# Scores of a batch's sixteen heads: fp32 matmuls of 64 rows, two heads side by side, in place of high and low parts

## The chip, the cores and the metric

The kernel runs on one core of one Trainium2 chip. The time is the device time of one execution in microseconds (us). Engines: PE (TensorE), DVE (VectorE), ACT (ScalarE), POOL (GpSimd) and SP (SyncE, which here only issues DMAs). PSUM is used as eight banks of 128 partitions x 512 fp32 numbers, named F0 to F3, S0, S1, TB and OB.

## The reference

Eight batches of 512 tokens x 128 channels go through two layers. The change touches only the last part, `_L1_ffn_ref`, an attention with 16 heads of 64 channels. Cut to what matters:

```python
q = jnp.einsum('btc,hdc->bhtd', x, Wq)
k = jnp.einsum('btc,hdc->bhtd', x, Wk)
...
v = jnp.einsum('bthe,bted->bhtd', mix_v, proj_v)
scores = jnp.einsum('bhid,bhjd->bhij', q * scale, k)
probs = jax.nn.softmax(scores, axis=-1)
attn = jnp.einsum('bhij,bhjd->bihd', probs, v)
...
res = jnp.einsum('bthe,bthd,efd->bthf', mask_o, attn, Wo)
return res.sum(axis=2)
```

Before it come, per batch, a linear attention with an MLP (`attn0`), eight dense experts (`moe_in`, `experts`), a causal attention with 8 heads (`attn1`) and the gates of this last part (`gates`).

## The kernel before, in words

Each engine runs its own program, and semaphores tie them. A program is a list of stages, each cut into marks; `schedule` walks a main stage's marks and puts marks of other stages beside them, in proportion. In the loop over batches two such walks follow each other. In the first, the **heads stage**, the 64 head steps of one batch (`heads`: 4 blocks of 128 query tokens x 16 heads) run beside `attn1` and `gates` of the next batch and `load`, `attn0` and `moe_in` of the one after. In the second, the **values stage**, `experts` runs beside the end of the heads (`finish`, `close`), the values and keys (`values`) and the first query steps (`begin`). The last batch has its values, and then its heads, with nothing beside them.

`head_steps` (line 63) writes the order of the steps: a *head* step per head and block, and other turns between them at places set by `QUERIES_AT`, `BACK_AT`, `MIXED_AT` and `RESULT_AT`:
- *queries* computes 128 tokens' queries of 8 heads into a bank (L971);
- *back* transposes 8 heads' results back (L984), DVE divides them (L1544), and after each second one SP sends them to DRAM (`out_rows`) and back in another layout (`onR`);
- two *mixed* turns (L991) add up the heads by their masks into `ymT` (L1209), and *result* (L997) multiplies by the output weights.

Every step but a rest takes the next of the two score banks S0 and S1 in turn (`TURN`). In `steps`, PE does at step k, in this order: the work of step k; for the head m of step k-2 the four transpositions of its exponentials `pr` into TB, called **T(m)** below (L719); and, if the head of step k-3 is odd, **AV** for that pair of heads (L1016), eight matmuls that alternate between the two column halves of OB, so that each head writes 64 partitions. ACT at step k first copies the transposed exponentials of step k-2 to `prT` (L1180), then computes the exponentials of head m, exp(m) (L1202). DVE gives it the negated maximum of the scores (L1529). Before PE fills a bank, it waits until what is in it has been read: for a head's scores, the exponential of the head two turns earlier.

A head's channels are 64 rows, but its score matmuls use all 128. Keys and queries are each split into a high part, rounded to fp32r, and a low part, the rest. One row half of `keys[:, h]` holds the high part and the other the low part of the same head. `q_high` holds the high part of the queries in both halves, `q_low` their low part in both, so two fp32r matmuls (L979 and L980) add up all four products:

```python
pe.matmul(bank_k[:, :], q_high[:, j % 3, h2, :], keys[:, h, :], start=True, stop=False)
pe.matmul(bank_k[:, :], q_low[:, j % 3, h2, :], keys[:, h, :], start=False, stop=True).then_inc(s_ps[0], 1)
```

For that, ACT copies the high part of the queries out of the bank (L1193, two copies of 64 rows), DVE subtracts it to give the low part (L1535, two), and two steps later ACT copies both parts to the other row half (L1186, four). For the keys, ACT copies the high part of two heads (L1147) and DVE subtracts into the other half (L1501), in each fourth mark of `values`, where DVE also multiplies (L1487) and adds up (L1495) the values. The experts' own DVE step is L1389, their matmuls L831, L834 and L839.

## Time and profile before

| what | value |
|---|---|
| median of 3 runs | 3120.25 us (3118.91 to 3121.88) |
| the profiled execution's own time | 3122.04 us |
| its span, first to last instruction | 3120.1 us |
| PE matmul busy | 2548.0 us, 82% |
| DVE, ACT, POOL busy | 1751.7, 1613.9, 788.4 us |
| mean granted clock of TensorE | 0.911 of 2.4 GHz |

The median is 1.8 us under the profiled execution, whose rows are used below. Busy time is the union of an engine's records; the ends of matmuls are modelled, so a busy PE need not be at its peak, and the distance between two starts says more than a duration. An fp32 matmul shows as two records, an fp32r matmul or an fp32 transposition as one.

### The profile page before, as it was taken

How to read it: one execution, taken by the hardware profiler on the slowest of the kernel's cores; microseconds unless marked ns; L12 is line 12 of the kernel's file. 1: busy time of each engine (PE TensorE's matmuls, PEld its weight loads, DVE VectorE, ACT ScalarE, POOL GpSimd, SP SyncE). 2: the span in 40 equal slices, each digit the busy share in tenths (PEclk: the TensorE clock that was granted, in tenths of full speed). 3: DMA queues.
4: the chain of work that ended last, by engine and by line, in shares of the span. 5: the costliest groups of instructions: out<-in, count | busy, mean ns of one | idle time of the engine just before them, and what ended most of it. 6: DMA issues, size and time to landing. Idle time of an engine off the chain costs nothing.

```text
span 3120.1 us, 44672 instructions
## 1 busy us (share of the span) xinstructions
PE 2548.0 (82%) x14892; PEld 1689.8 (54%) x14892; DVE 1751.7 (56%) x2906; ACT 1613.9 (52%) x3329; POOL 788.4 (25%) x370
## 2 busy tenths in 40 slices
PE   3984698789797997889787897979979797996487
PEld 2453347664476545765376644765457553774265
DVE  4235763547645494465935567364854649447732
ACT  0241246663566636664366635666366643774474
POOL 1003520106401181013601055011810127004500
PEclk7996799999898998999999998999989999998698
DMA  2110010102001120012101020011200121001001
GB/s 73 47 41 8 10 51 1 55 14 76 12 15 41 41 59 2 15 55 55 32 1 47 22 65 22 9 48 41 59 2 15 48 55 38 15 15 39 0 28 31
DMA packets 210739, 101.63 MB, mean 33 GB/s; under 512 B 137367, under 2 KB 189620, under 8 KB 210492
## 3 DMA queue, kind: packets, MB, share of 16 engines
q1 hardware_dynamic: 205052, 95.74, 11.1%
q10 hardware_dynamic: 5440, 2.75, 0.3%
q8 instruction: 136, 2.23, 0.3%
q14 instruction: 111, 0.91, 0.1%
HBM read 77.48 MB, written 20.99 MB: 32 GB/s over the span
## 4 chain that ended last, share of the span: by engine, by line
PE 61%; DVE 14%; issue 14%; ACT 8%; POOL 2%; DMA 1%; DVEq 0%; ACTq 0%; POOLq 0%; SPq 0%
PE bank L719 9%; PE bank L834 6%; PE bank L1016 6%; PE bank L831 6%; PE bank L839 6%; PE bank L871 5%; PE bank L979 4%; PE bank L887 4%; PE bank L980 3%; DVE vals L1495 2%; PE bank L997 2%; ACT pr L1202 2%; DVE prod L1487 2%; DVE nrm_o L1304 2%; DVE nmax L1529 1%
## 5 line engine op out<-in xcount | busy, mean ns | idle before, releaser
L704 POOL TENSOR_TENSOR prod<-pv,mixv 128x1024 f32<-128x1024 f32 x184 | 589.8, 3234 | 305.4 <-ACT pv L1141 157.1
L1529 DVE TENSOR_REDUCE nmax<-bank 128x1 f32<-128x512 f32 x512 | 351.0, 690 | 539.9 <-PE bank L980 519.3
L1202 ACT ACTIVATE pr<-bank,nmax 128x512 f32<-128x512 f32 x512 | 350.7, 685 | 189.3 <-DVE nmax L1529 187.6
L1180 ACT ACTIVATE prT<-bank 128x512 f32<-128x512 f32 x512 | 305.0, 596 | 258.0 <-PE bank L719 251.8
L643 POOL TENSOR_TENSOR rstd<-vareps,minus_half 128x4 f32<-128x4 f32 x48 | 50.0, 1043 | 1495.5 <-DVE vareps L1299 1495.4
L1083 ACT ACTIVATE arena<-bank 128x512 f32<-128x512 f32 x256 | 152.8, 597 | 444.3 <-PE bank L831 397.3
L979 PE MATMUL bank<-keys,q_high 128*128 128x512 f32 x512 | 267.6, 523 | 113.3 <-DVE on L1544 30.9
L719 PE MATMUL bank<-ident,pr 128*128 128x128 f32 x2048 | 327.1, 284 | 29.0 <-ACT prT L1180 28.6
L719 PEld LDWEIGHTS bank<-ident,pr 128*128 128x128 f32 x2048 | 256.9, 146 | 118.8 <-ACT prT L1180 41.9
L1495 DVE TENSOR_REDUCE vals<-prod 128x128 f32<-128x1024 f32 x256 | 306.9, 1209 | 11.7 <-POOL prod L704 10.8
L834 PE MATMUL bank<-h1T,Wu 128*128 128x512 f32 x512 | 272.1, 614 | 40.0 <-DVE arena L1389 39.9
L1016 PE MATMUL bank<-prT,vals 128*64 128x128 f32 x4096 | 299.2, 290 | 5.6 <-ACT prT L1180 5.6
L1389 DVE TENSOR_TENSOR arena<-bank,arena 128x512 f32<-128x512 f32 x256 | 175.0, 688 | 218.7 <-PE bank L834 192.8
L839 PE MATMUL bank<-arena,Wd 128*128 128x512 f32 x512 | 273.4, 620 | 27.0 <-DVE arena L1389 27.0
L831 PE MATMUL bank<-h1T,Wg 128*128 128x512 f32 x512 | 269.0, 607 | 3.9 <-ACT h1T L1048 3.9
L1417 DVE TENSOR_REDUCE nmax<-bank 128x1 f32<-128x128 f32 (+3 forms) x256 | 125.1, 491 | 251.1 <-PE bank L872 250.5
L1016 PEld LDWEIGHTS bank<-prT,vals 128*64 128x64 f32 x4096 | 234.4, 143 | 55.3 <-issue 40.7
L871 PE MATMUL bank<-arena,attT 128*128 128x512 f32 (+3 forms) x512 | 203.7, 482 | 14.3 <-ACT arena L1111 12.9
L980 PE MATMUL bank<-keys,q_low 128*128 128x512 f32 x512 | 214.3, 419 | 0.0
L979 PEld LDWEIGHTS bank<-keys,q_high 128*128 128x128 f32 x512 | 102.4, 200 | 189.3 <-ACT pr L1202 61.0
L834 PEld LDWEIGHTS bank<-h1T,Wu 128*128 128x128 f32 x512 | 97.3, 195 | 173.2 <-issue 105.9
L1487 DVE TENSOR_TENSOR prod<-pv,mixv 128x1024 f32<-128x1024 f32 x72 | 187.4, 2603 | 0.0
(226 smaller groups left out, 3878.0 us busy)
## 6 DMA issues: line engine op xcount, KB each, us to landing
Wg<-in_L_ffn_Wg SPq DMA_DIRECT2D x64, 256.0 KB, 2.9
Wu<-in_L_ffn_Wu SPq DMA_DIRECT2D x64, 256.0 KB, 3.5
Wd<-in_L_ffn_Wd SPq DMA_DIRECT2D x64, 256.0 KB, 3.9
out_rows<-on SPq DMA_DIRECT2D x32, 512.0 KB, 2.6
onR<-out_rows SPq DMA_DIRECT2D x32, 512.0 KB, 3.9
xin<-in_L_attn_x SPq DMA_DIRECT2D x8, 256.0 KB, 4.3
mask_rows<-masko SPq DMA_DIRECT2D x8, 256.0 KB, 4.6
maskR<-mask_rows SPq DMA_DIRECT2D x8, 256.0 KB, 6.6
```

Source lines behind the costliest of these rows:

```text
L704: g.tensor_tensor(*value_piece(n), ALU.mult).then_inc(vprod_r[0], 1)
L719: last = pe.transpose(dst[:, i * P:(i + 1) * P], src(i), ident[:, :])
L831: pe.matmul(F0[:, :], Wg[:, e % 2, j * P:(j + 1) * P], hbT[:, :], start=True, stop=True).then_inc(gu_g[0], 1)
L834: pe.matmul((F2, F3)[n % 2][:, :], Wu[:, e % 2, j * P:(j + 1) * P], hbT[:, :], start=True, stop=True).then_inc(gu_u[0], 1)
L839: pe.matmul(F1[:, :], Wd[:, e % 2, j, :], act[:, m % 3, :], start=(m == 0), stop=(m == n_all - 1)).then_inc(down_ps[0], 1)
L871: pe.matmul(f[:, 0:w], q1T[:, i * P:(i + 1) * P], k1z[:, h, 0:w], start=True, stop=False, skip_group_check=True)
L979: pe.matmul(bank_k[:, :], q_high[:, j % 3, h2, :], keys[:, h, :], start=True, stop=False)
L980: pe.matmul(bank_k[:, :], q_low[:, j % 3, h2, :], keys[:, h, :], start=False, stop=True).then_inc(s_ps[0], 1)
L1016: last = pe.matmul(OB[DS * odd:DS * odd + DS, at:at + P], vals[:, j, h - 1 + odd, :], prT[:, (m - 1 + odd) % 3, j * P:(j + 1) * P], start= ...
L1202: s.activation(pr[:, x % 2, :], bank_k[:, :], ACT.Exp, bias=nmax[:, x % 2:x % 2 + 1], accum_out=den[:, i % 2, h:h + 1]).then_inc(s_out[0], 1)
L1495: v.tensor_reduce(vals[:, i, HQ * q:HQ * q + HQ, :], prod[:, m % NPROD, :].rearrange("p (h d e) -> p h d e", h=HQ, e=NE), X_AXIS, ALU.add) ...
L1529: v.tensor_reduce(nmax[:, m % 2:m % 2 + 1], (S0, S1)[turn % 2][:, :], X_AXIS, ALU.max, negate=True).then_inc(nmax_r[0], 1)
```

## The change

It drops the high and low parts. `keys` now has one row half per head (fp32, 8 pairs of heads), `qs` likewise, so that both are plain copies of a bank of 128 rows. The scores of heads 2p and 2p+1 are one fp32 matmul each of 64 contraction rows, on the upper and the lower row half, the first into one score bank and the second into the other. PE issues both at the step of the even head, after it has waited for both banks; the step of the odd head issues no scores. The constants of the order change too.

```diff
-QUERIES_AT = (8, 11)
-BACK_AT = (13, 5)
-MIXED_AT = (9, 10)
+QUERIES_AT = (4, 8)
+BACK_AT = (14, 6)
+MIXED_AT = 10
...
-        keys = sb("keys", [P, HS, T], F32R)
-        q_high = sb("q_high", [P, 3, HS // 2, P], F32R)
-        q_low = sb("q_low", [P, 3, HS // 2, P], F32R)
+        keys = sb("keys", [P, NP, T])
+        qs = sb("qs", [P, 3, NP // 2, P])
...
+                    if kind == "head":
+                        for odd in range(0 if x % 2 else 2):
+                            free(b, turn + odd)
+                    elif kind != "rest":
+                        free(b, turn)
...
-                        pe.matmul(bank_k[:, :], q_high[:, j % 3, h2, :], keys[:, h, :], start=True, stop=False)
-                        pe.matmul(bank_k[:, :], q_low[:, j % 3, h2, :], keys[:, h, :], start=False, stop=True).then_inc(s_ps[0], 1)
+                    if kind == "head" and x % 2 == 0:
+                        i, p = x // HS, x % HS // 2
+                        j, r = 2 * i + p // (NP // 2), p % (NP // 2)
+                        if r == 0:
+                            wait(pe, s_out, b, COPIED[STEP_AT["queries", j]])
+                        for odd in range(2):
+                            half = slice(DS * odd, DS * odd + DS)
+                            pe.matmul((S0, S1)[(turn + odd) % 2][:, :], qs[half, j % 3, r, :], keys[half, p, :], start=True, stop=True).then_inc(s_ps[0], 1)
...
-                        for odd in range(2):
-                            r = DS * odd
-                            s.activation(keys[r:r + DS, 2 * p + odd, :], (TB, OB)[p % 2][r:r + DS, :], ACT.Copy).then_inc(kh_r[0], 1)
+                        s.activation(keys[:, p, :], (TB, OB)[p % 2][:, :], ACT.Copy).then_inc(keys_r[0], 1)
...
-                        for part in (q_high, q_low):
-                            for odd in range(2):
-                                last = s.activation(other_half(part, x, odd), own_half(part, x, odd), ACT.Copy)
-                        last.then_inc(q_both[0], 1)
...
-                        for odd in range(2):
-                            last = s.activation(own_half(q_high, x, odd), queries_of(bank_k, odd), ACT.Copy)
-                        last.then_inc(s_out[0], 1)
+                        s.activation(qs[:, x % 3, :, :].rearrange("p a t -> p (a t)"), bank_k[:, :], ACT.Copy).then_inc(s_out[0], 1)
...
-                            last = v.tensor_tensor(keys[DS - r:2 * DS - r, 2 * p + odd, :], (TB, OB)[p % 2][r:r + DS, :], keys[r:r + DS, 2 * p + odd, :], ALU.subtract)
...
-                            last = v.tensor_tensor(own_half(q_low, m, odd), queries_of((S0, S1)[turn % 2], odd), own_half(q_high, m, odd), ALU.subtract)
```

`free(b, turn)` is the wait for the bank's earlier contents, as before but without the low part. DVE now handles a *back* turn ahead of the maximum of the same step, not behind it. Lines of the changed kernel have other numbers.

PE, heads stage of the last batch, two heads in a row before the change (L719 is T, L1016 is AV):

```order
L979 MATMUL bank<-keys,q_high 128x512
L980 MATMUL bank<-keys,q_low 128x512
L719 MATMUL bank<-ident,pr 128x128 x4
L979 MATMUL bank<-keys,q_high 128x512
L980 MATMUL bank<-keys,q_low 128x512
L719 MATMUL bank<-ident,pr 128x128 x4
L1016 MATMUL bank<-prT,vals 64x128 x8
```

The same place after it (L972 scores, L705 T, L1008 AV, L976 a turn back):

```order
L972 MATMUL bank<-keys,qs 128x512 x2
L705 MATMUL bank<-ident,pr 128x128 x4
L1008 MATMUL bank<-prT,vals 64x128 x8
L705 MATMUL bank<-ident,pr 128x128 x4
L972 MATMUL bank<-keys,qs 128x512 x2
L705 MATMUL bank<-ident,pr 128x128 x4
L1008 MATMUL bank<-prT,vals 64x128 x8
L705 MATMUL bank<-ident,pr 128x128 x4
L976 MATMUL bank<-ident,oaT 128x128 x4
```

Scores stood between the two transpositions; now only AV does, and both heads' scores stand together.

SP, first DMAs of the heads stage inside the loop, before (`out_rows` and `onR` are the head rows of blocks 0 and 1, `xin` and `rows` belong to the load of a later batch):

```order
L578 DMA out_rows<-on 128x1024
L281 ISA
L580 DMA onR<-out_rows 128x16x64
L281 REGISTER_ALU
L578 DMA out_rows<-on 128x1024
L281 REGISTER_ALU
L580 DMA onR<-out_rows 128x16x64
L281 REGISTER_ALU
L554 ISA
L554 DMA xin<-in_L_attn_x 128x4x128
L557 ISA
L557 DMA rows<-row_table 128x384
```

And after:

```order
L564 DMA out_rows<-on 128x1024
L280 ISA
L566 DMA onR<-out_rows 128x16x64
L280 REGISTER_ALU
L540 ISA
L540 DMA xin<-in_L_attn_x 128x4x128
L543 ISA
L543 DMA rows<-row_table 128x384
```

The load, with the first two experts' weights behind it, now stands ahead of the head rows of block 1, since that block's second turn back comes one head later and the load's mark now stands beside it; DVE first uses it a head later.

DVE, values stage, a mark with keys before:

```order
L1487 TENSOR_TENSOR prod<-pv,mixv 128x1024
L1495 TENSOR_REDUCE vals<-prod 128x128
L1501 TENSOR_TENSOR keys<-bank,keys 64x512 x2
L1389 TENSOR_TENSOR arena<-bank,arena 128x512 x2
L1495 TENSOR_REDUCE vals<-prod 128x128
```

And after:

```order
L1467 TENSOR_TENSOR prod<-pv,mixv 128x1024
L1475 TENSOR_REDUCE vals<-prod 128x128
L1369 TENSOR_TENSOR arena<-bank,arena 128x512 x2
L1475 TENSOR_REDUCE vals<-prod 128x128
L1369 TENSOR_TENSOR arena<-bank,arena 128x512
```

The two subtractions ahead of the experts' step L1389, now L1369, are gone.

## Rows read from the trace of the kernel before

**Rows 1.** The page: busy time by engine, and the chain that ended last by engine

```profile
PE 2548.0 (82%) x14892; PEld 1689.8 (54%) x14892; DVE 1751.7 (56%) x2906; ACT 1613.9 (52%) x3329; POOL 788.4 (25%) x370
...
PE 61%; DVE 14%; issue 14%; ACT 8%; POOL 2%; DMA 1%; DVEq 0%; ACTq 0%; POOLq 0%; SPq 0%
```

**Rows 2.** Windows: start:end, length, busy us of each engine, granted clock, DMA

```profile
core 0: us, PE busy (x) PEld busy (x) DVE busy (x) ACT busy (x) POOL busy (x), PEclk, DMA share, GB/s
1184.00:1427.00 243.00, 206.77 (x1525) 159.15 (x1526) 118.89 (x258) 159.46 (x343) 21.67 (x18) 0.92 0.08 23
1427.00:1550.00 123.00, 106.38 (x330) 49.33 (x329) 94.85 (x95) 43.47 (x75) 77.69 (x25) 0.97 0.21 55
...
2935.00:3095.00 160.00, 130.82 (x1076) 100.58 (x1076) 63.59 (x99) 109.94 (x247) 0.00 (x0) 0.93 0.07 21
...
1209.00:1282.00 73.00, 67.33 (x477) 52.73 (x476) 28.19 (x54) 47.97 (x111) 0.00 (x0) 0.93 0.01 1
```

**Rows 3.** Timeline, last heads stage: start us, us, engine, line, what [idle before <-releaser]

```profile
2972.41 0.69 ACT L1202 ACTIVATE pr<-bank,nmax 128x512 f32<-128x512 f32 x1 [1.19 <-DVE nmax L1529]
...
2973.24 0.50 PE L979 MATMUL bank<-keys,q_high 128*128 128x512 f32 x1 [0.69 <-ACT pr L1202]
...
2973.82 0.63 PE L719 MATMUL bank<-ident,pr 128*128 128x128 f32 x4
...
2974.38 1.09 PE L1016 MATMUL bank<-prT,vals 128*64 128x128 f32 x16
2974.49 0.60 ACT L1180 ACTIVATE prT<-bank 128x512 f32<-128x512 f32 x1
2974.98 0.68 ACT L1202 ACTIVATE pr<-bank,nmax 128x512 f32<-128x512 f32 x1
...
2975.40 0.50 PE L979 MATMUL bank<-keys,q_high 128*128 128x512 f32 x1
...
2975.97 0.60 PE L719 MATMUL bank<-ident,pr 128*128 128x128 f32 x4
2976.33 0.48 PE L979 MATMUL bank<-keys,q_high 128*128 128x512 f32 x1
...
2977.35 0.63 PE L719 MATMUL bank<-ident,pr 128*128 128x128 f32 x4 [0.31 <-ACT prT L1180]
...
2979.86 0.48 PE L979 MATMUL bank<-keys,q_high 128*128 128x512 f32 x1
```

**Rows 4.** Groups by line, last heads stage: busy us, mean ns | idle before

```profile
L1186 ACT ACTIVATE q_high<-q_high 64x512 fp32r<-64x512 f32 x14 | 8.8, 628 | 2.7 <-DVE q_low L1535 2.7
...
L1193 ACT ACTIVATE q_high<-bank 64x512 fp32r<-64x512 f32 x12 | 7.0, 586 | 0.1
...
L1535 DVE TENSOR_TENSOR q_low<-bank,q_high 64x512 fp32r<-64x512 f32 x14 | 9.6, 686 | 0.5 <-ACT q_high L1193 0.3
```

**Rows 5.** Groups by line, values stage 1427 to 1550, DVE

```profile
L1501 DVE TENSOR_TENSOR keys<-bank,keys 64x512 fp32r<-64x512 f32 x16 | 11.0, 688 | 0.4
```

**Rows 6.** The chain by line: values stages 697 to 819, 2524 to 2644, 2842 to 2935

```profile
by line: PE bank L834 21.5%; PE bank L839 20.0%; PE bank L831 19.1%; issue 10.8%; PE bank L935 4.2%; DVE prod L1487 3.8%; DVE vals L1495 3.6%; DVE arena L1389 2.5%; DVE keys L1501 2.3%; PE bank L927 2.1%; PE bank L1016 1.7%; PE bank L971 1.
...
by line: PE bank L834 18.8%; PE bank L831 16.5%; PE bank L839 14.5%; issue 14.2%; DVE vals L1495 8.3%; DVE keys L1501 4.8%; DVE arena L1389 4.5%; DVE prod L1487 4.3%; PE bank L935 2.9%; PE bank L1016 1.7%; PE bank L991 1.7%; PE bank L997 1.
...
by line: DVE prod L1487 29.7%; DVE vals L1495 26.6%; issue 17.5%; DVE keys L1501 6.2%; PE bank L991 3.9%; PE bank L1016 2.3%; PE bank L997 2.2%; PE bank L921 1.9%; DVE q_low L1535 1.5%; PE bank L719 1.3%; PE bank L935 1.2%; ACT prT L1180 1.
```

**Rows 7.** Waits of the whole run: us in total, times, longest us

```profile
PE bank L991 <- DVE q_low L1535: 57.8, 15, 7.8
...
DVE stats L1291 <- DMA rows<-row_table: 42.0, 7, 6.9
```

**Rows 8.** The chain in order of time, values stage: start us, us, what

```profile
1070.68 0.86 PE bank L834 x2
```

**Rows 9.** Timeline of PE: two result turns in heads stages

```profile
3085.32 2.05 PE L997 MATMUL bank<-WoG,ymT 64*128 64x128 f32 x16
...
3004.25 3.38 PE L997 MATMUL bank<-WoG,ymT 64*128 64x128 f32 x16 [1.81 <-ACT pr L1202]
```

More of the change, by code:

```diff
@@ L80, in head_steps @@
             steps.append(("back", 2 * i - 1))
-        if i >= 1 and h in MIXED_AT:
-            steps.append(("mixed", 2 * (i - 1) + MIXED_AT.index(h)))
+        if i >= 1 and h == MIXED_AT:
+            steps += [("mixed", 2 * (i - 1)), ("mixed", 2 * i - 1)]
         if i >= 1 and h == RESULT_AT:
@@ L942, in heads @@
             def heads(b):
-                wait(pe, ks_r, b, NP)
+                wait(pe, keys_r, b, NP)
                 yield from steps(b, BEGIN, FINISH_AT)
@@ L950, in close, with free @@
                 yield from steps(b, CLOSE_AT, len(HEAD_STEPS) + 1)
+            def free(b, turn):
+                if turn > 2:
+                    before = TURN.index(turn - 2)
+                    what, y = HEAD_STEPS[before]
+                    if what == "result":
+                        wait(pe, xout_r, b, y + 1)
+                    elif what == "back":
+                        wait(pe, on_r, b, y + 1)
+                    else:
+                        wait(pe, s_out, b, COPIED[before])
             def steps(b, first, end):
@@ L957, in steps @@
                     bank_k = (S0, S1)[turn % 2]
-                    if kind != "rest" and turn > 2:
-                        before = TURN.index(turn - 2)
-                        what, y = HEAD_STEPS[before]
-                        if what == "result":
-                            wait(pe, xout_r, b, y + 1)
-                        elif what == "back":
-                            wait(pe, on_r, b, y + 1)
-                        else:
-                            wait(pe, s_out, b, COPIED[before])
-                        if what == "queries":
-                            wait(pe, ql_r, b, y + 1)
+                    if kind == "head":
[3 more added lines that the diff above has]
+                        free(b, turn)
                     if kind == "queries":
@@ L1495, in values @@
                         v.tensor_reduce(vals[:, i, HQ * q:HQ * q + HQ, :], prod[:, m % NPROD, :].rearrange("p (h d e) -> p h d e", h=HQ, e=NE), X_AXIS, ALU.add).then_inc(vals_r[0], 1)
-                    if n % 4 == 3:
-                        p = n // 4
-                        for odd in range(2):
-                            r = DS * odd
-                            wait(v, kh_r, b, 2 * p + odd + 1)
-                            last = v.tensor_tensor(keys[DS - r:2 * DS - r, 2 * p + odd, :], (TB, OB)[p % 2][r:r + DS, :], keys[r:r + DS, 2 * p + odd, :], ALU.subtract)
-                        last.then_inc(ks_r[0], 1)
                     yield n + 1
@@ L1523, in steps @@
                         v.tensor_tensor(xout[:, m, :], (S0, S1)[TURN[k - 1] % 2][:, 0:P], xout[:, m, :], ALU.add).then_inc(xout_r[0], 1)
-                    kind, m, turn = step_of(k)
-                    if kind == "head":
-                        wait(v, s_ps, b, turn)
-                        if m >= 2:
-                            wait(v, s_out, b, COPIED[STEP_AT["head", m - 2]])
-                        v.tensor_reduce(nmax[:, m % 2:m % 2 + 1], (S0, S1)[turn % 2][:, :], X_AXIS, ALU.max, negate=True).then_inc(nmax_r[0], 1)
-                    kind, m, turn = step_of(k - 1)
-                    if kind == "queries":
-                        wait(v, s_out, b, COPIED[k - 1])
-                        for odd in range(2):
-                            last = v.tensor_tensor(own_half(q_low, m, odd), queries_of((S0, S1)[turn % 2], odd), own_half(q_high, m, odd), ALU.subtract)
-                        last.then_inc(ql_r[0], 1)
                     kind, m, turn = step_of(k - 1)
```

29 lines of the change are left out of this document (8 added, 21 removed).

## The prediction

> **What bounds the kernel now.** I read four views in this order. The page: PE is busy for 82% of the span and holds 61% of the chain that ended last; no other engine passes 56% [rows 1]. The windows by stage then split a batch in two [rows 2]. In the heads stage (243 us, 1184 to 1427) the 64 head steps of one batch run beside the attention of the next: PE busy 206.8, ACT 159.5, DVE 118.9. In the values stage (123 us, 1427 to 1550) the experts run beside values and keys: PE 106.4, DVE 94.9. Seven batches have both; the last has its values alone (2842 to 2935) and its heads alone (160 us, PE 130.8). PE is thus the first limit in both, and what it waits for decides the rest.
>
> Third, the timeline of the heads alone gives one undisturbed pair of heads [rows 3]: from the scores at 2976.33 to those at 2979.86 it is 3.53 us, and PE waits 0.31 of it. The two score matmuls of a head hold PE for 0.57 us there (2975.40 to 2975.97). Fourth, groups, chain and waits show what stands around such a pair [rows 4 to 9].
>
> **What the change removes.**
> *Queries.* A query step now costs ACT two copies out of the bank and four between the halves: in the last heads stage 12 copies out of the bank, 7.0 us, 14 between the halves of q_high, 8.8 us, and as many of q_low, so 24.6 us, and DVE has 14 subtractions, 9.6 us [rows 4]. One copy of 128x512 stays, 0.60 us as the prT copy is in rows 3. So ACT loses 24.6 - 6 x 0.6 = 21 us and DVE 9.6 us per heads stage. Neither is the limit there, so nothing is credited for busy time; what counts is that steps wait for them, below.
> *Keys.* 16 subtractions on DVE, 11.0 us, go per values stage [rows 5], and ACT's 16 copies of 64 rows become 8 of 128, which are hidden either way, since ACT stands idle there for most of the time [rows 2]. On DVE a product, a sum and then this pair (1.4 us) stand in a row, and the experts' own DVE step behind them, for which PE waits. The chain holds the keys for 2.3 to 4.8% of six values stages, mean 3.6% of 122 us = 4.4 us each, and 6.2% of the last 93 us = 5.8, with q_low 1.4 more [rows 6]. Sum: 6 x 4.4 + 2 for the first stage, in whose row the keys aren't listed, + 7 = **-35 us**. Bounds: nothing if the sums of L1495 are simply late next, and 8 x 11.0 = -88 if all of DVE's time was paid.
> *A load moved.* SP's order in front.md shows the next batch's loads now ahead of the second transfer of head rows, not behind it. Before, DVE waited for the rows of this load 42.0 us in 7 waits, 6.0 each, with a maximum and q_low queued behind it, and PE's L991 waited 57.8 us for q_low in 15 waits [rows 7]. The loads need nothing of the second transfer, so they are issued right behind the first transfer, many head steps earlier. 6 loop passes x 6 = **-36 us**; bounds 0 (the row transfer that is now issued behind them is as late) and -57.8.
>
> **What it adds.**
> *The score matmuls.* An fp32 matmul of 512 columns is 0.86 us of PE [rows 8]. Two of them stand for four fp32r ones, 2 x 0.57. The trace has no two matmuls in different row halves. The nearest row is L1016, whose 16 records alternate between two column halves and take 1.09 us, where the 16 records of L997, all in the same place, of the same 128 columns, take 2.05 [rows 3, 9]: halves run side by side. I take that for rows too, so a pair's scores hold PE 0.86 us, and bound it by 1.72 (one after the other). The Trainium skill (TensorE: Matmul & The Clock Gate, Packing small matmuls) also says that different row groups run concurrently, but gives 3.07x for four row tiles, not 4x; by that share, as an estimate, a pair would be 1.12 us and the sum up to 65 us higher.
> *Changes of shape.* A transposition that follows scores in the same shape starts them 0.36 after its own start (2975.97, 2976.33); before AV it is 0.56 (2973.82, 2974.38), and AV to scores is 1.02, where 16 records of 2.05/16 in two halves would be free after 8 x 0.11 = 0.9 [rows 3, 9]. So a change of shape costs 0.15 to 0.25 us. A pair had two; now the scores have a shape of their own and it has four: +0.3 to +0.5 us, part of it inside a wait. The Trainium skill (TensorEngine Tiling (Array Packing), Key Properties) says that changing the tiling mode drains the engine; the row agrees, and it speaks against the change.
> *A new wait.* Scores of head m waited for the exponential of head m-2; now both of a pair wait until both banks are free, so for head m-1, the one just before. With the durations of [rows 3, 8], from the pair's start at 0: scores end 1.05; T(m-2) 1.06 to 1.69; AV 1.62 to 2.71; ACT copies T(m-2) 1.7 to 2.3 and starts exp(m) at 2.2 (maximum of m ready at 1.8). T(m-1) starts 1.02 behind AV, 2.64 to 3.27; its copy 3.31 to 3.91; ACT starts an exponential 0.50 behind the copy's start, so exp(m+1) is 3.81 to 4.50; PE resumes 0.14 later, **4.64 us** for a pair against 3.53, with PE idle from 3.1 on. Queued behind that wait are the next transpositions and AV, and in the heads stage the next batch's own matmuls.
>
> The other turns shrink for the same reason. The last heads stage is 32 x 3.53 = 113 us and 47 for 22 other turns. Now a query's four matmuls (0.9) fit into the 1.5 us of idle, its one copy delays the pair by about 1.2, but the next pair then has only one transposition in front (3.7 instead of 4.6): net 0.2. The same for the turns back. A group of two mixed turns and a result I walk at 5.1 (two of 1.1, one of 2.0, their copies, less the idle). That is 13 x 0.2 + 3 x 5.1 = 18. So 149 + 18 = 167 against 160: **+6 us** for the heads alone. Bounds: -20 (the turns cost nothing and bubbles fill) and +36 (no turn gets cheaper).
> *Beside attention.* In 1209 to 1282 PE is busy 67.3 of 73 [rows 2], two of the other stage's steps stand between any two head steps, and the exponential is done when PE comes to the pair: 8 pairs pay only the shape changes, +2. The other 24 are as alone, +4.5. ACT's table loads now meet the chain, the next batch's matmuls fill some idle; I let them cancel to -1.5: **+5 us** per stage, +35 for seven. Bounds -10 and +25 each.
>
> **Sum.** -35 - 36 + 6 + 35 = -30 us against the profiled execution's 3122.0 (span 3120.1), so 3092; the median of the runs is 1.8 lower, so I say **3090 us**.
>
> **Rivals.**
> (a) *The wait is paid in full.* PE stands at the pair in 24 of 32 pairs of every batch, 1.1 us each, and the other turns save only half of what I credit (29 us less half): +1.1 x 32 - 15 = +21 alone, and per stage beside +17 (24 x 1.1 less 9): 21 + 119 - 71 = +69, **3190 us**. It decides from the point where a transposition of the odd head is followed by less than about 1.5 us of other PE work, which is so wherever no inner attention step lies there. For it: PE must wait in order. Against: before, stalls of the queries' copies (q_low, on, ACT pr before L979) took similar time.
> (b) *The row halves run one after the other.* +0.86 us on the chain of each of 256 pairs: +220, **3310 us**. For it: no row shows row halves together; against: the column halves.
> (c) *The copies and subtractions cost more than the chain shows.* Values stages come down from 122 towards their 106 to 109 us of PE: 10 us each instead of 4.4, and the heads stages lose another 5 each: **3010 us**. For it: PE is idle for 17 of the 123 us [rows 2], and DVE, which it waits for, is the engine relieved.
> (d) *PE's clock.* After a wait of 1.81 us L997 took 3.38 us instead of 2.05 [rows 9]: part of it ran at the lower level, 1.2 GHz. With 1.5 us idle in each pair's 4.6 that may come more often. At 1 us lost in every 15 us of the heads that are as alone (167 + 7 x 125 = some 1,040 us): +70, **3160 us**. [...]
>
> **The numbers.** Forecast (3040 to 3125) 0.44, (a) 0.24, (b) 0.10, (c) 0.12, (d) 0.10. Faster by over 0.2% (6 us, what a measurement here can tell from no change) is (c) and most of the forecast: 0.12 + 0.37 = 0.49. Same 0.05 of the forecast and 0.02 of (d): 0.07. Slower: the rest, 0.44. The range leaves out (b) and the lower end of (c) and reaches over (a): 3005 to 3215. The forecast's own range is 3040 to 3125.
>
> **What would show it.** L979 and L980 become one line with 1024 records, pairs of them starting together; if the pairs start one after the other, it is (b). A clean pair of the last heads stage takes 4.6 us, PE's wait before it released by ACT's pr, about 1.5 us. The DVE wait for the rows' DMA and L991's wait for q_low are gone. Values stages of 117 to 119 us; heads stages beside attention within 6 us of 243, the last one 160 to 172. A mean granted clock under 0.88 points to (d). I am wrong if the pair's period in the last stage is under 4 or over 5 us, or if the values stage doesn't shorten.

## The result and the profile after

The changed kernel takes **3135.56 us** (median of 12 runs, 3128.95 to 3138.36) against 3121.74 for the kernel before (12 runs, 3118.91 to 3132.31): ratio 1.0036, 95% interval 1.0025 to 1.0047. It is slower by more than the 0.2% that can be told here. The prediction was 3090 us and leaned to faster: it was wrong in its sign. The time lies in the wide range that also covers rival (a), 3005 to 3215, and 11 us above the forecast's own, 3040 to 3125. The profiled execution has a span of 3135.8 us, 15.7 more than before.

The page of the changed kernel, for [rows 1]; first busy time by engine, then groups (busy us, mean ns | idle before the group, and its releaser):

```profile
PE 2562.2 (82%) x14892; PEld 1580.7 (50%) x14892; DVE 1557.9 (50%) x2650; ACT 1389.2 (44%) x2957; POOL 806.5 (26%) x370
...
L972 PE MATMUL bank<-keys,qs 64*128 64x512 f32 x1024 | 315.8, 694 | 201.3 <-ACT pr L1182 95.2
...
L1008 PE MATMUL bank<-prT,vals 128*64 128x128 f32 x4096 | 301.5, 293 | 59.1 <-ACT prT L1169 59.1
```

The change did what it says: DVE lost 194 us of work and ACT 225. PE has as many records as before, is busy 14 us more, and stands 201 us in front of the scores (L972). In the kernel before it stood this long there and in front of AV:

```profile
L979 PE MATMUL bank<-keys,q_high 128*128 128x512 f32 x512 | 267.6, 523 | 113.3 <-DVE on L1544 30.9 <-ACT pr L1202 29.8 <-DVE q_low L1535 21.7
L980 PE MATMUL bank<-keys,q_low 128*128 128x512 f32 x512 | 214.3, 419 | 0.0
L1016 PE MATMUL bank<-prT,vals 128*64 128x128 f32 x4096 | 299.2, 290 | 5.6 <-ACT prT L1180 5.6
```

The busy times of L979 and L980 overlap, so they can't be added: the window of the whole run for what reads `keys` gives PE 390.7 us for both together, against 315.8 now. From a pair's first score to what follows, two heads took 2 x 0.57 = 1.14 us and take 1.06. So the scores became a little cheaper, and the waits ahead of them and of AV grew by 88 and 53.5 us. The windows of the changed kernel, for [rows 2] (same columns):

```profile
1185.00:1433.00 248.00, 209.12 (x1523) 144.10 (x1524) 106.26 (x244) 139.97 (x310) 21.54 (x18) 0.93 0.07 22
1433.00:1549.00 116.00, 106.03 (x331) 49.33 (x329) 82.83 (x78) 35.58 (x61) 80.70 (x25) 1.00 0.22 58
```

The values stage fell from 123 to 116 us, with PE's 106 us of work now near its length; the heads stage rose from 243 to 248. In the last batch the first pair now stands among the values, at 2916.8; from the start of the last sum into vals (2944.3) to the last score (3110.9) it is 166.6 us, where the kernel before took 159.2. The timeline of the one pair of the last heads stage that has nothing else between its scores and the next, for [rows 3]:

```profile
3076.54 1.13 PE L972 MATMUL bank<-keys,qs 64*128 64x512 f32 x4 [1.45 <-ACT pr L1182]
3077.60 0.66 PE L705 MATMUL bank<-ident,pr 128*128 128x128 f32 x4
3077.67 1.29 DVE L1510 TENSOR_REDUCE nmax<-bank 128x1 f32<-128x512 f32 x2 [3.28 <-PE bank L972]
3078.19 1.09 PE L1008 MATMUL bank<-prT,vals 128*64 128x128 f32 x16
...
3079.21 0.66 PE L705 MATMUL bank<-ident,pr 128*128 128x128 f32 x4
...
3079.90 0.60 ACT L1169 ACTIVATE prT<-bank 128x512 f32<-128x512 f32 x1
3080.40 0.68 ACT L1182 ACTIVATE pr<-bank,nmax 128x512 f32<-128x512 f32 x1
3080.97 0.20 ACT L1182 ACTIVATION_READ_ACCUMULATOR pr<-bank,nmax 128x1 f32 x1
...
3081.32 1.13 PE L972 MATMUL bank<-keys,qs 64*128 64x512 f32 x4 [1.45 <-ACT pr L1182]
```

Four records (two heads, two passes each) take 1.13 us, and the next matmul starts 1.06 us after them: the row halves run together. The pair takes 4.78 us, and PE waits 1.45 for the odd head's exponential, nearly as walked. The waits of [rows 7]: L983 (then L991) no longer waits for DVE, and the wait for rows is one of 5.3 us:

```profile
PE bank L983 <- DMA onR<-out_rows: 7.6, 1, 7.6
DVE stats L1271 <- DMA rows<-row_table: 5.3, 1, 5.3
```

All stages of all profiled runs, in us, read from first and last starts of lines. "Start" is the time to the first score. "Heads" runs from a batch's first score to the first gate matmul of the experts, and "values" from there to the next first score, each the sum over six loop passes. "7th" runs from first to last score of the heads stage that has attention beside it but no load. "Last values" ends at the last sum into vals, and "alone" is the rest, the last heads stage. The two columns at the right are the granted clock of TensorE, averaged over the six heads and the six values stages.

| kernel | start | heads x6 | values x6 | 7th | last values | alone | span | clock, heads | clock, values |
|---|---|---|---|---|---|---|---|---|---|
| before | 453.3 | 1462.8 | 727.9 | 198.6 | 92.3 | 185.2 | 3120.1 | 0.927 | 0.950 |
| after | 456.2 | 1504.6 | 678.7 | 223.3 | 81.5 | 191.6 | 3135.8 | 0.927 | 0.998 |
| b_new_order | 459.1 | 1433.3 | 724.0 | 213.9 | 90.7 | 187.8 | 3108.8 | 0.938 | 0.949 |
| b_back_only | 459.3 | 1452.5 | 725.0 | 206.7 | 90.9 | 191.4 | 3125.8 | 0.925 | 0.959 |
| keys_dve | 457.0 | 1501.9 | 717.9 | 224.6 | 90.8 | 192.4 | 3184.6 | 0.932 | 0.967 |
| one_by_one | 456.7 | 1477.5 | 684.9 | 224.2 | 81.9 | 183.4 | 3108.6 | 0.958 | 0.989 |
| one_old_order | 452.0 | 1498.4 | 681.7 | 213.1 | 80.6 | 191.9 | 3117.7 | 0.945 | 0.996 |
| one_pass | 454.7 | 1413.8 | 681.2 | 204.2 | 83.4 | 180.7 | 3018.0 | 0.887 | 0.994 |
| exp_odd_first | 456.7 | 1497.4 | 679.4 | 222.1 | 81.6 | 189.6 | 3126.8 | 0.936 | 0.997 |
| exp_first | 453.7 | 1527.7 | 679.0 | 224.3 | 84.4 | 205.9 | 3175.1 | 0.951 | 0.996 |
| four_bufs | 455.7 | 1504.8 | 678.3 | 224.4 | 81.4 | 191.3 | 3135.9 | 0.926 | 0.998 |
| split_wait | 453.5 | 1444.1 | 680.7 | 216.1 | 81.5 | 192.6 | 3068.5 | 0.955 | 0.994 |
| split_last_single | 456.3 | 1442.0 | 679.5 | 215.9 | 81.3 | 182.0 | 3057.0 | 0.957 | 0.995 |
| split_odd | 451.1 | 1449.5 | 681.9 | 213.8 | 81.5 | 187.6 | 3065.4 | 0.951 | 0.993 |

Before to after: values -49 and -11, heads +42 and +25, alone +6, start +3. The start varies by 8 us from kernel to kernel without following their edits, so nothing of 3 us is read from it.

The clock columns matter below, and what the clock costs can be estimated: at the 1.2 GHz level PE's work takes up to twice as long (in rows further down AV takes 1.97 us in place of 1.09), so half of PE's busy time at that level counts as lost. By the clock records in the traces that is, over the whole run, 179 us before, 164 after, 138 in one_by_one and 126 in split_wait; in the seven heads stages beside attention it is 95, 113, 73 and 68, and 87 in b_new_order; in the six values stages 26 before and 1 after.

### The profile page after: what moved, and what is told of

Same layout as the page of the kernel before. It is cut to its first block and busy times, and to the rows that moved or that the text cites. A ratio compares the mean times of both kernels' runs of the same rounds, so it can differ in the third digit from the quotient of the medians.

```text
span 3135.8 us, 43928 instructions
## 1 busy us (share of the span) xinstructions
PE 2562.2 (82%) x14892; PEld 1580.7 (50%) x14892; DVE 1557.9 (50%) x2650; ACT 1389.2 (44%) x2957; POOL 806.5 (26%) x370
## 5 line engine op out<-in xcount | busy, mean ns | idle before, releaser
L1510 DVE TENSOR_REDUCE nmax<-bank 128x1 f32<-128x512 f32 x512 | 342.8, 686 | 677.6 <-PE bank L972 677.2
L690 POOL TENSOR_TENSOR prod<-pv,mixv 128x1024 f32<-128x1024 f32 x184 | 598.7, 3291 | 274.4 <-ACT pv L1133 169.9
L972 PE MATMUL bank<-keys,qs 64*128 64x512 f32 x1024 | 315.8, 694 | 201.3 <-ACT pr L1182 95.2
L1182 ACT ACTIVATE pr<-bank,nmax 128x512 f32<-128x512 f32 x512 | 350.0, 685 | 207.6 <-DVE nmax L1510 207.4
L705 PE MATMUL bank<-ident,pr 128*128 128x128 f32 x2048 | 362.8, 304 | 38.8 <-ACT prT L1169 38.8
L705 PEld LDWEIGHTS bank<-ident,pr 128*128 128x128 f32 x2048 | 246.3, 153 | 261.8 <-issue 205.1
L1008 PE MATMUL bank<-prT,vals 128*64 128x128 f32 x4096 | 301.5, 293 | 59.1 <-ACT prT L1169 59.1
L1008 PEld LDWEIGHTS bank<-prT,vals 128*64 128x64 f32 x4096 | 237.1, 145 | 127.0 <-ACT prT L1169 70.6
L1369 DVE TENSOR_TENSOR arena<-bank,arena 128x512 f32<-128x512 f32 x256 | 174.7, 684 | 243.5 <-PE bank L820 216.4
L825 PE MATMUL bank<-arena,Wd 128*128 128x512 f32 x512 | 260.4, 593 | 6.7 <-DVE arena L1369 6.7
L972 PEld LDWEIGHTS bank<-keys,qs 64*128 64x128 f32 x1024 | 84.6, 198 | 262.4 <-ACT pr L1182 114.4
L1097 ACT ACTIVATE arena<-bank 128x128 f32<-128x128 f32 (+3 forms) x256 | 112.1, 438 | 128.1 <-PE bank L705 127.3
```

The source lines that it names most:

```text
L690: g.tensor_tensor(*value_piece(n), ALU.mult).then_inc(vprod_r[0], 1)
L705: last = pe.transpose(dst[:, i * P:(i + 1) * P], src(i), ident[:, :])
L825: pe.matmul(F1[:, :], Wd[:, e % 2, j, :], act[:, m % 3, :], start=(m == 0), stop=(m == n_all - 1)).then_inc(down_ps[0], 1)
L972: pe.matmul((S0, S1)[(turn + odd) % 2][:, :], qs[half, j % 3, r, :], keys[half, p, :], start=True, stop=True).then_inc(s_ps[0], 1)
L1008: last = pe.matmul(OB[DS * odd:DS * odd + DS, at:at + P], vals[:, j, h - 1 + odd, :], prT[:, (m - 1 + odd) % 3, j * P:(j + 1) * P], start= ...
L1182: s.activation(pr[:, x % 2, :], bank_k[:, :], ACT.Exp, bias=nmax[:, x % 2:x % 2 + 1], accum_out=den[:, i % 2, h:h + 1]).then_inc(s_out[0], 1)
```

## The experiments

**The two parts of the change apart.** The kernel before with the new order of steps alone (high and low parts kept):

```diff
-QUERIES_AT = (8, 11)
-BACK_AT = (13, 5)
-MIXED_AT = (9, 10)
+QUERIES_AT = (4, 8)
+BACK_AT = (14, 6)
+MIXED_AT = 10
```

> The kernel before with only the changed constants of the order (queries at 4 and 8, turns back at 14 and 6, both mixed turns at 10), high and low parts kept. My term for the load that moved ahead of the second transfer of head rows says -36 us (6 per pass), so 3080 to 3100, with DVE's wait for the rows' DMA down from 42 us to under 10. Rival: the stall was only the place where other lateness showed, and the time stays within 10 us of before, or rises because the queries' copies now fall at worse places.

3109.49 us, ratio 0.9948 (0.9932 to 0.9965), faster, but not as far as the 3080 to 3100 that I expected. The six loop passes become 29.5 us shorter in the heads, but the 7th stage 15.3 longer. By the spans (one execution each) the order is worth -11.3 us and the rest of the change +27.1: scores, keys and queries together, with DVE's earlier turns back, cost time, although values and keys became shorter. The order alone also has a wait of its own, for the low parts that now are wanted sooner; before it was 21.7 us, and in the changed kernel there is none:

```profile
PE bank L979 <- DVE q_low L1535: 93.4, 42, 4.9
```

*Where the load's gain is.* Only the turns back are moved:

```diff
-BACK_AT = (13, 5)
+BACK_AT = (14, 6)
```

> The kernel before with only the turns back moved (14 and 6 for 13 and 5), which is enough to put the load ahead of the second transfer of head rows in SP's order. Load theory: the loop's heads stages fall from about 244 to 238 us, all of the order's gain, and the heads stage that has no load beside it stays at 206, so the time is below that of the whole new order: 3085 to 3100. Rival: the other moves bring the gain, and the time stays within 6 us of before.

3131.16 us, ratio 1.0022 (1.0003 to 1.0040): a miss. Its waits say why:

```profile
PE bank L991 <- DMA onR<-out_rows: 38.0, 14, 7.4
...
DVE stats L1291 <- DMA rows<-row_table: 5.4, 1, 5.4
```

The wait for the load is gone as expected (42.0 to 5.4), but the second turn back is now one head later with the mixed step still at 9, and PE waits for the head rows' transfer, 38.0 us where it was one wait of 7.5. The six heads stages gain 10.3 us in place of 29.5. The rest needs the other moves too, which b_new_order has.

*The keys.* After, with the two subtractions per key pair put back on DVE (their result is not used):

```diff
+                    if n % 4 == 3:
+                        p = n // 4
+                        wait(v, kc_r, b, p + 1)
+                        for odd in range(2):
+                            r = DS * odd
+                            last = v.tensor_tensor(spare[DS - r:2 * DS - r, :], (TB, OB)[p % 2][r:r + DS, :], keys[r:r + DS, p, :], ALU.subtract)
+                        last.then_inc(keys_r[0], 1)
```

> The changed kernel with two DVE subtractions of 64x512 per pair of keys put back (written to a spare tile), PE's next keys waiting for them as before. If the 8.2 us that each values stage gained (11 in the last) are DVE's subtractions, the stages go back from 113.5 to about 121 us and the time rises by 55 to 70 us, to 3190 to 3205. If the gain came from ACT's shorter copies or from the queries, it rises by less than 20.

3186.35 us, ratio 1.0179 (1.0159 to 1.0198), 51 above after and just under the 3190 to 3205 expected: values +39.2 for six, +9.3 for the last. Most of the values stages' gain is DVE's. The clock of the six stages falls with it, from 0.998 to 0.967.

**The pair.** *Scores one by one.* After, with each head's fp32 score at its own step and a wait for its own bank only. The row halves then never run together:

```diff
-                    if kind == "head":
-                        for odd in range(0 if x % 2 else 2):
-                            free(b, turn + odd)
-                    elif kind != "rest":
+                    if kind != "rest":
...
-                    if kind == "head" and x % 2 == 0:
+                    if kind == "head":
...
-                        for odd in range(2):
+                        for odd in (x % 2,):
```

> The changed kernel, but each head's scores stand at its own step again and wait for their own bank alone, so the wait for both banks is gone and the two row halves never run together. Wait theory: in the heads alone the period stays about the same (4.4 to 4.8 us a pair), since what the wait gives back the second 0.86 us and two more changes of shape take; beside attention, where PE is the bound, each pair pays 1.0 to 1.3 us: +7 to 7 x 35, so 3250 to 3380. If the wait alone were dear and the side-by-side run of the halves worth little, it would fall below 3136.

3097.37 us, ratio 0.9901 (0.9885 to 0.9917): my expectation was wrong by over 150 us, and the kernel beats both. Its score group, as on the page:

```profile
L969 PE MATMUL bank<-keys,qs 64*128 64x512 f32 x1024 | 590.7, 667 | 46.7 <-ACT pr L1179 30.0
```

PE works 275 us more on scores than after, and still the time falls by 38. So 1.06 us of scores put on PE per pair costs less than the joint wait; I had priced PE's work as if it stood behind waits that stayed. Of the idle time, 155 us are gone ahead of the scores, and the 59.1 ahead of AV are 1.4, since a score now stands between a head's transpositions and AV. PE's idle time falls by 247.5 us in all (573.6 to 326.1), less than the scores add. What is left is the clock, 0.933 in place of 0.923: 26 us by the estimate above, where the spans differ by 27. With the old order of steps it is one_old_order:

> Each head's fp32 scores on its own row half at its own step (as in one_by_one), with the order of the kernel before (queries at 8 and 11, turns back at 13 and 5, mixed turns at 9 and 10). Against before this is the pure exchange of four half products for one fp32 matmul, without pairs and without the new order. If the order is worth 16 us here as it was for high and low parts (3109 against 3126), this gives 3110 to 3120, with DVE's wait for the rows' DMA back at about 40 us. If the order works only together with the high and low parts, it stays at 3097 within 8 us.

3121.51 us (ratio 0.9987, 0.9963 to 1.0010), but its 12 runs lie between 3102 and 3150, so only its median is used, which can't be told from before and lies 24 us above one_by_one: the new order helps this form as well.

*Shorter scores.* After, with keys and queries as fp32r, so one pass in place of two; the low parts are left out of the scores:

```diff
-        keys = sb("keys", [P, NP, T])
-        qs = sb("qs", [P, 3, NP // 2, P])
+        keys = sb("keys", [P, NP, T], F32R)
+        qs = sb("qs", [P, 3, NP // 2, P], F32R)
```

> The changed kernel with keys and queries rounded to fp32r and no low parts at all, so the scores are products of rounded numbers; pairs, waits and order are those of the change. A pair's scores take one pass of some 0.25 to 0.5 us instead of 1.06. Wait theory: the shorter pass stands on the chain from one pair's exponential to the next, so each of 256 pairs gains about 0.5 us or more, in the heads alone (191 us) as beside attention: -130 to -160, 2975 to 3005. If PE's standing at the pair swallowed it, the gain would be under 60.

3016.09 us, ratio 0.9652 (0.9635 to 0.9669), 119 less than after, 0.47 per pair, a little under what I expected. From the pair's start to what follows it is 0.43 us where it was 1.06. With the pair together and one wait for both banks, most of the score time is on the path: everything behind the wait begins later by it.

*The exponential that PE waits for, earlier.* First for the odd head alone, with four buffers for pr:

```diff
-                    if kind == "head":
+                    if kind == "head" and not (step_of(k)[0] == "head" and step_of(k)[1] % 2):
...
+                        before_k, m_k, _ = step_of(k - 2)
+                        if before_k == "head" and (step_of(k)[0] == "head" and step_of(k)[1] % 2):
+                            wait(s, p_T, b, m_k + 1)
+                            s.activation(prT[:, m_k % 3, :], TB[:, :], ACT.Copy).then_inc(pT_r[0], 1)
```

> The changed kernel with four buffers for the exponentials in place of two, and with ACT computing the odd head's exponential before it copies the even head's transposition of the pair before, not behind it. The work is the same. If the new wait is what the heads stages pay (PE stands until exp of the odd head is done, and that stands on ACT behind a copy that waits for PE's last transposition), a clean pair falls from about 4.5 us to about 3.7, PE's wait for ACT pr before the scores from 1.45 to under 0.5, and the time by 80 to 130 us, to 3005 to 3055. If instead PE's own work (shape changes, fp32 passes) is what is paid, the time stays within 10 us of 3136.

3128.78 us, ratio 1.0010 (0.9997 to 1.0023). The undisturbed pair fell from 4.78 to 4.10 us, PE's wait in it from 1.45 to 0.78:

```profile
3068.53 1.13 PE L972 MATMUL bank<-keys,qs 64*128 64x512 f32 x4 [0.71 <-ACT pr L1182]
...
3072.63 0.70 PE L972 MATMUL bank<-keys,qs 64*128 64x512 f32 x2 [0.78 <-ACT pr L1182]
```

But the total fell only by 7, the stage alone by 2.0, and six heads stages together by 7.2. (The 4.57 us of the expectation was a pair with two transposition groups and no AV between; such a pair fell to 3.83.) The wait that I could shorten is a small part of what the pair costs: in the six loop heads stages PE waits 129.9 us ahead of the scores, and 42.7 of it for the exponential. The same for every head:

> Four buffers for the exponentials, and ACT computes the exponential of every head before it copies the transposition of two steps earlier. Both exponentials of a pair are then done 3.2 us after its scores start, and PE should find both banks free, but the second transposition waits for the first one's later copy. I expect a clean pair at 3.8 to 4.1 us and 3115 to 3135 in all, no better than exp_odd_first (3129); a gain of more than 20 us over it would say that the banks' wait was still the limit there.

3179.73 us, ratio 1.0181 (1.0161 to 1.0201): a miss in the other direction. The wait moved to AV, which needs the copy that is now late:

```profile
L972 PE MATMUL bank<-keys,qs 64*128 64x512 f32 x1024 | 302.8, 667 | 147.2 <-ACT pr L1182 51.8
L1008 PE MATMUL bank<-prT,vals 128*64 128x128 f32 x4096 | 291.0, 286 | 154.4 <-ACT prT L1186 153.0
```

54 us less ahead of the scores, 95 more ahead of AV. It has the longest waits of all kernels here and still a clock of 0.951 in the heads stages, above the changed kernel's 0.927. The buffers themselves (`pr` of four in place of two):

> After, with four buffers for the exponentials in place of two and nothing else: a control for the two runs that changed the order on ScalarE and had four buffers too. In the last stage the exponentials never waited for a transpose in the rows that I read, so 3130 to 3140 (no change). If the buffers alone bring something, the 7 us of the run with the odd head's exponential first was theirs: 3124 to 3130.

3134.64 us, ratio 1.0029 (1.0016 to 1.0042): nothing.

*The wait in two parts.* After, in the same order on every engine; PE waits for the even bank, issues the even score, then waits for the odd bank:

```diff
-                    if kind == "head":
-                        for odd in range(0 if x % 2 else 2):
-                            free(b, turn + odd)
-                    elif kind != "rest":
+                    if kind != "rest" and not (kind == "head" and x % 2):
                         free(b, turn)
...
                             half = slice(DS * odd, DS * odd + DS)
+                            if odd:
+                                free(b, turn + 1)
```

> After, with the pair's wait in two parts: the even head's score goes as soon as its own bank is free, the odd head's directly behind it when its bank is free. TensorE still stands at the same place until the odd bank is free. If what costs is that TensorE stands in its program order (and all matmuls of the other stage behind it), the total stays within 10 us of the changed kernel's 3135.6, so 3125 to 3145. If what costs is that two softmaxes begin at once and VectorE and ScalarE get their work in bursts, the early start of the even head takes half of the 38 us away that the pairing costs against one by one (3097.4): 3110 to 3122.

**3070.45 us** (3068.46 to 3075.62), ratio 0.9835 (0.9816 to 0.9855): 65 less than after by one wait's place. It is beyond what either theory gave. Its groups on the page:

```profile
L971 PE MATMUL bank<-keys,qs 64*128 64x512 f32 x1024 | 425.3, 671 | 74.2 <-ACT pr L1181 44.4
```

127 us of idle time ahead of the scores are gone; 110 us more are spent in the scores. In the heads stage at 1516 to 1755, the two scores of 14 of 32 pairs still start within 0.1 us of each other; where the odd bank is late, the even score fills the wait. That alone frees PE no earlier, as the expectation said: in the 85 pairs at full clock whose odd score starts 0.9 us or more behind the even one, PE goes on 1.05 us after the odd score's start, as it would behind a joint wait. Two other things changed. The even head's maximum starts earlier, and ACT waits for maxima 165.6 us in place of 207.4. And the clock of the six heads stages is 0.955 in place of 0.927, worth some 40 of their 60.5 us by the estimate above; by the spread within a kernel it is less (after: 3138 us at 0.923, 3129 at 0.930; one_by_one: 3112 at 0.931, 3092 at 0.940), so 0.935 against 0.923 over the run may be 15 to 40 of the 65 us. In heads stages it is 60.5 us, in the 7th 7.2; alone it brings nothing.

One piece of the program shows both kernels at the same place. The timeline of PE in the changed kernel, and in a second fence its window from 1676.05 to 1684.57 (columns as in [rows 2]):

```profile
1676.53 0.66 PE L705 MATMUL bank<-ident,pr 128*128 128x128 f32 x4
1678.85 1.66 PE L972 MATMUL bank<-keys,qs 64*128 64x512 f32 x4 [1.66 <-DVE xout L1496]
1680.44 1.11 PE L705 MATMUL bank<-ident,pr 128*128 128x128 f32 x4
1682.24 1.97 PE L1008 MATMUL bank<-prT,vals 128*64 128x128 f32 x16 [0.69 <-ACT prT L1169]
1684.14 1.12 PE L976 MATMUL bank<-ident,oaT 128*128 128x128 f32 x4
```

```profile
1676.05:1684.57 8.52, 6.17 (x35) 3.82 (x35) 5.09 (x7) 3.13 (x9) 1.20 (x1) 0.69 0.00 0
```

And the same piece, timeline and window, with the wait in two parts:

```profile
1642.32 0.66 PE L705 MATMUL bank<-ident,pr 128*128 128x128 f32 x4
1642.90 2.25 PE L971 MATMUL bank<-keys,qs 64*128 64x512 f32 x4
1645.08 0.66 PE L705 MATMUL bank<-ident,pr 128*128 128x128 f32 x4
1646.42 1.09 PE L1007 MATMUL bank<-prT,vals 128*64 128x128 f32 x16 [0.69 <-ACT prT L1168]
1647.45 0.66 PE L975 MATMUL bank<-ident,oaT 128*128 128x128 f32 x4
```

```profile
1642.20:1647.82 5.62, 4.93 (x33) 2.65 (x32) 5.09 (x7) 2.64 (x7) 0.33 (x1) 1.00 0.00 0
```

The pair follows a result step, whose bank DVE has to read (xout, L1496). The joint wait stands 1.66 us for it, though the other bank is free. Behind the wait PE's granted clock is lower: a transposition group takes 1.11 in place of 0.66 and AV 1.97 in place of 1.09, so part of this stretch ran at the 1.2 GHz level (granted clock 0.69 over it). With the even score in the wait, the clock stays at 1.00, and the piece is 2.9 us shorter. The even exponential gains nothing by itself here: in both kernels it starts 0.49 us behind the copy of the transposition, and that comes after the odd score. From PE's first score behind the bank's release to the turn back it is 5.29 us against 3.42 (1644.03, where the odd score starts, to 1647.45), the same work, so some 1.9 of the 2.9 us are the clock. Over these heads stages (1549 to 1798 and 1516 to 1755) it is 0.92 with the joint wait and 0.96 with the split one. That the wait itself brings the clock down is not shown: exp_first waits longest and keeps 0.951.

*The odd exponential again,* now on the split wait:

> The version with the pair's wait in two parts (3070.5), and on ScalarE the odd head's exponential ahead of the copy of the transposed exponentials (four buffers). With one wait for both banks that order brought 7 us, because it freed the second bank earlier. If that bank still holds TensorE, the gain repeats: 3060 to 3066. If with the split wait the second bank is no longer what decides, no change or a little worse because the copies are later: 3068 to 3076.

3072.59 us, ratio 0.9831 (0.9812 to 0.9849): no gain, as the second branch said. The second bank no longer decides.

*The better version.* One by one was 8 us faster in the last stage alone, so there each score stays at its own step, and the split wait elsewhere:

```diff
+                    alone = isinstance(b[0], int) and b[0] + b[1] == NB - 1
-                    if kind != "rest" and not (kind == "head" and x % 2):
+                    if kind != "rest" and (alone or not (kind == "head" and x % 2)):
...
-                    if kind == "head" and x % 2 == 0:
+                    if kind == "head" and (alone or x % 2 == 0):
...
-                        for odd in range(2):
+                        for odd in (x % 2,) if alone else range(2):
                             half = slice(DS * odd, DS * odd + DS)
-                            if odd:
+                            if odd and not alone:
```

> The version with the pair's wait in two parts (3070.5), and in the last heads stage alone each head's score at its own step, one by one. There the one-by-one kernel took 240.5 us from the stage before to the last score, the split one 248.4 and the changed kernel 248.7. The stages are apart, so the two gains add: 3060 to 3066. If the 8 us came from the state of the earlier stages instead, it stays at 3068 to 3074.

**3062.58 us** (3055.24 to 3064.82), ratio 0.9794 (0.9773 to 0.9815), the fastest that computes all that the kernel before does. The last stage went from 192.6 to 182.0 us, the other stages stayed, and the gains add.

## Why the prediction was wrong

*Score pair and clean pair: right.* Row halves together (rival b is out), scores that hold PE 1.06 us with one change of shape (walked 1.05), the walk's times within 0.1 (second transposition at 2.67, walked 2.64; the odd exponential at 3.86, walked 3.81), PE's wait 1.45 (walked some 1.5), the pair 4.78 where I had 4.64: the odd exponential starts 0.05 us later than walked, and ACT's read of its accumulator, a record of 0.20 us, ends 0.09 behind it before the bank counts as free, which the walk left out. The estimate from the Trainium skill (TensorE: Matmul & The Clock Gate, Packing small matmuls) of 1.12 us per pair is near the 1.13 of the record group, but not for its reason: one head's score alone also holds PE 1.05 us, so two halves show no loss. Here is the timeline of one_by_one:

```profile
2974.27 1.12 PE L969 MATMUL bank<-keys,qs 64*128 64x512 f32 x2
2975.32 0.66 PE L705 MATMUL bank<-ident,pr 128*128 128x128 f32 x4
```

The walk's 1.05 was right as a sum and wrong in its parts: it took 0.86 for the matmul and the rest for the change of shape behind it. In the single records at full clock, the two passes of one 64-row score start 0.53 us apart (474 of 485 in one_by_one), with no change of shape between them, where those of the experts' matmuls start 0.43 apart. So the 64-row matmul itself takes longer; why is not shown. The change of shape shows ahead of the scores: they start 0.20 us after the start of the last transposition's record, where the 128-row ones of the kernel before start 0.03 after it if nothing holds them.

*Heads alone, +6: right in size, in part by luck.* +6.4, the cheaper other turns included. But the clock of this stage went from 0.90 to 0.95, for which the walk had no term; by the estimate above it gave back some 7 us. The windows of the stage, before and then after:

```profile
2934.90:3120.10 185.20, 142.26 (x1168) 110.57 (x1168) 66.44 (x104) 114.54 (x256) 0.00 (x0) 0.90 0.09 25
2944.30:3135.80 191.50, 136.61 (x1164) 92.84 (x1164) 54.52 (x90) 93.38 (x222) 1.09 (x1) 0.95 0.08 24
```

*Keys, -35: mis-sized.* Values stages lost 60.0 us against before, and putting the subtractions back costs 48.5 of it in those stages. 49.2 are in the six loop stages, 8.2 each; the step took 4.4 from the chain's share of the keys. About half of the 8.2 is idle time of PE (4.0 each, near the 4.4), and the other half is less busy time for the same work: the clock of these stages went from 0.950 to 0.998. The step had no term for that. Rival (c), at 10 us a stage, was near it here, but the heads stages did not follow it.

*The load moved, -36: near in size, but not the load's alone, and with a cost that I had not seen.* -29.5 over the six passes from the order alone, and DVE's wait for the rows went from 42.0 to 5.3. But b_back_only has the load moved too and gains 10.3. The whole order also ends L991's wait of 57.8 us for q_low and lengthens L979's from 21.7 to 93.4 us, so -29.5 is what is left of several waits, and its nearness to -36 is in part luck. And the same order costs 15.3 us in the 7th stage, where no load stands beside it. The windows of that stage, before:

```profile
2644.00:2842.60 198.60, 176.61 (x1454) 139.18 (x1453) 98.61 (x179) 143.35 (x324) 14.57 (x12) 0.98 0.06 17
```

and with the new order alone:

```profile
2616.40:2830.30 213.90, 186.59 (x1458) 143.60 (x1456) 99.47 (x179) 145.65 (x327) 15.01 (x12) 0.94 0.05 16
```

The same work keeps PE busy 10 us longer, at a clock of 0.94 in place of 0.98, and the other 5 are idle time. b_back_only already has 8.1 of the 15.3 us, so about half comes with the turns back; the queries and the mixed turns were not tried apart.

*Beside attention, +5 per stage, +35: the step that failed most.* Against the kernel with the same order, the heads stages grew by 71.3 and 9.4 us, 11.5 each, more than twice the 5. The step let 8 of 32 pairs pass without a wait, priced the others by the clean pair, and cancelled the rest to -1.5. In the six loop stages at most 95 of 192 pairs wait, half and not three quarters, so the count was too high; but three things were not in it. The wait for both banks falls not only on the previous head's exponential: of the 201.3 us ahead of L972 that is 95.2, of which one wait of 29.7 stands in the last values stage, and 90.2 are for what stands in the banks at other turns (on, qs, ymT, xout). I had these turns only in the stage alone, and as cheaper. With the split wait these 90.2 are 10.2. AV waits for the copy (59.1 us against 5.6), since the pair's scores no longer stand in between; the split wait leaves that at 58.6, so it is no part of the 65 us. And PE loses more to the clock, 113 us in the seven stages against 87 with the same order, by the estimate above. Against that stands a gain that the step had not counted: L979's waits for q_low, 71.8 us of these six stages in b_new_order, are gone. The split wait, which takes off only the joint wait, leaves +10.8 and +2.2 against the same order: of the +80.7, only 13.0 had to be paid. What DVE's earlier turns back do was not tried apart.

*Sum.* Values -54.5 and the order -19.7 (loops -29.5, 7th +15.3, values -5.5), alone +6.4, beside attention +80.7, start +2.9: +15.8, which is the difference of the spans but for rounding. Rival (a) had the right mechanism and place, and more than its size. It gave +17 per stage beside attention, measured 11.5, and +21 alone, measured 6.4. Its chance of 0.24 was too low: "the exponential is done when PE comes" was an assumption for dense stretches, not read from a row, and no row of other turns stood beside it. Rival (d), the clock, can't be read from the mean, which even rose, from 0.911 to 0.923. By stages it went both ways: up in the values and in the heads alone, and down against the same order in the heads beside attention (0.938 to 0.927 in six). I looked for it in the wrong stage, and what moves it stays open.

## What to carry to other kernels

When two matmuls can run together, let each wait for its own bank, in issue order: the first and what reads it then start early, and the two still overlap where both banks are free. That one wait's place was worth 65 us of 3136, more than pairing or not pairing. Price a joint wait by everything that ever stands in both resources, not by the steady state of the cleanest stretch. And set the granted clock of each stage beside its waits, before and after: here it carried half of the keys' gain in the loop and, by the estimate, nearly all of what one_by_one gains over the changed kernel, while the mean of the run hid it.

## What was not expected of the hardware

Two fp32 matmuls of 64 contraction rows and 512 columns in the two row halves take the time of one head's, 1.05 to 1.06 us to the next start, without a loss that the trace shows. Each of the two passes of such a matmul takes 0.53 us, where one of 128 rows takes 0.43. And a PE that does 220 us more work (2782.5 busy in one_by_one against 2562.2 in after) can end 27 us earlier in the profiled executions, with the clock at 0.933 in place of 0.923.
